# Mamba block with gated FFN on one core: Silu in one instruction and in a burst, the norms' scale on ScalarE, another order on every engine

## What is computed

```
xz = x @ W_xproj.T                     # 64 rank columns, 16 of B, 16 of C
dt = softplus(xz[:64] @ W_dt.T + b_dt)
h_t = exp(dt*A) * h_{t-1} + dt*x*B     # 16 states per channel, a scan over time
y   = sum_s h*C + Dp*x
x1  = layernorm(x + y)
out = layernorm(x1 + (silu(x1 @ Wg.T) * (x1 @ Wu.T)) @ Wd.T)   # 768 hidden columns
```

## Time and profile before

| | |
|---|---|
| median of three executions | 2001.36 us |
| span of the profiled execution | 2000.0 us |
| busy: TensorE, VectorE, ScalarE, GpSimd | 1767, 1828, 1569, 1702 us |
| granted TensorE clock, mean | 0.953 of full |
| moved by DMA | 215.35 MB, 108 GB/s mean |

### The profile page before, as it was taken

The page is one execution under the profiler, slowest core; times in us unless marked ns, Lnnn a source line. Parts: engine busy times, 40 slices in busy tenths (PEclk is TensorE's granted clock), DMA queues, the critical chain, the costliest instruction groups (busy, mean ns, idle before and its releaser), DMA issues.

```text
span 2000.0 us, 37094 instructions
## 1 busy us (share of the span) xinstructions
PE 1766.9 (88%) x11048; PEld 1388.2 (69%) x11048; DVE 1828.2 (91%) x2285; ACT 1568.7 (78%) x2924; POOL 1701.9 (85%) x779
## 2 busy tenths in 40 slices
PE   6788989988899988889888989889989888899886
PEld 3666777676777767777666767667767667777764
DVE  4899999999999999999999999999999999999994
ACT  6878878788877878787788787888777787787862
POOL 5998888988888988889888888988889888889880
PEclk9899999999999999999999999999999999999999
DMA  7233233233233233233233333233333332332300
GB/s 242 89 109 118 94 119 123 90 122 117 86 119 126 87 119 117 96 117 127 85 122 104 110 117 115 97 120 98 117 117 101 111 116 87 117 133 70 122 12 21
DMA packets 116565, 215.35 MB, mean 108 GB/s; under 512 B 11153, under 2 KB 45554, under 8 KB 116466
## 3 DMA queue, kind: packets, MB, share of 16 engines
q1 hardware_dynamic: 116466, 214.40, 32.7%
HBM read 195.48 MB, written 18.87 MB: 107 GB/s over the span
## 4 chain that ended last, share of the span: by engine, by line
PE 51%; issue 19%; DVE 15%; ACT 11%; POOL 2%; DVEq 1%; ACTq 0%; DMA 0%; POOLq 0%; SPq 0%
PE p_o L1005 16%; PE p_y L960 9%; DVE h L705 8%; PE p_m L992 6%; PE p_da L934 5%; PE p_c L943 3%; PE p_m L906 3%; DVE hid L749 3%; PE p_m L914 3%; ACT p_da L539 2%; PE p_m L982 2%; ACT da_k L539 2%; ACT L539 2%; DVE silu_g L743 2%; DVE h L713 1%
## 5 line engine op out<-in xcount | busy, mean ns | idle before, releaser
L422 POOL TENSOR_TENSOR h<-h,c_bc 128x1024 f32<-128x1024 f32 x352 | 832.2, 2368 | 147.6 <-ACT h_carry L525 119.8
L412 POOL TENSOR_TENSOR ub<-u,b_bc 128x1024 f32<-128x1024 f32 x320 | 756.8, 2370 | 0.1
L960 PE MATMUL p_y<-ident,h 128*128 128x128 f32 x4096 | 535.6, 278 | 3.3 <-DVE h L713 2.2
L960 PEld LDWEIGHTS p_y<-ident,h 128*128 128x128 f32 x4096 | 479.9, 144 | 38.5 <-issue 16.4
L539 ACT ACTIVATE p_da<-dt,neg_a 128x512 f32<-128x512 f32 x640 | 432.1, 682 | 86.7 <-DVE h L705 82.8
L705 DVE TENSOR_TENSOR_SCAN h<-p_da,ub 128x512 f32<-128x512 f32 x320 | 380.4, 1210 | 37.9 <-ACT p_da L539 27.4
L705 DVE TENSOR_TENSOR_SCAN h<-p_da,h_carry,ub 128x512 f32<-128x512 f32 x320 | 399.2, 1269 | 11.0 <-ACT p_da L539 10.3
L553 ACT ACTIVATE ub_t<-u_t,bc_t 128x256 f32<-128x256 f32 x768 | 344.9, 497 | 27.7 <-issue 26.9
L1005 PE MATMUL p_o<-wt_down,hid 128*128 128x256 f32 x1536 | 354.7, 381 | 11.8 <-DVE hid L749 8.6
L934 PE MATMUL p_da<-ident,ub_t 128*128 128x128 f32 x1536 | 242.7, 295 | 132.6 <-DVE h L705 131.8
L1005 PEld LDWEIGHTS p_o<-wt_down,hid 128*128 128x128 f32 x1536 | 284.4, 190 | 67.8 <-issue 29.6
(11 more groups left out here) (101 smaller groups left out, 1819.6 us busy)
## 6 DMA issues: line engine op xcount, KB each, us to landing
c_bc<-bc_rows_dram SPq DMA_DIRECT2D x352, 256.0 KB, 4.9
b_bc<-bc_rows_dram SPq DMA_DIRECT2D x128, 512.0 KB, 5.3
x_in<-in_L_attn_x SPq DMA_DIRECT2D x32, 512.0 KB, 3.5
b_bc<-bc_rows_dram SPq DMA_DIRECT2D x64, 256.0 KB, 3.1
out_x<-res_n SPq DMA_DIRECT2D x32, 512.0 KB, 3.3
bc_rows_dram<-bc_rows SPq DMA_DIRECT2D x32, 64.0 KB, 1.6
hid<-in_L_ffn_w_gate SPq DMA_DIRECT2D x1, 768.0 KB, 5.0
hid<-in_L_ffn_w_up SPq DMA_DIRECT2D x1, 768.0 KB, 6.8
```

Source lines behind the costliest of these rows:

```text
L412: nc.gpsimd.tensor_tensor(ub[:, i % UB_SLOTS, :, :], u[:, par, :, :], b_bc[:, i:i + 1, :].broadcast_to([P, DH, T]), ALU.mult).then_inc(s_u ...
L422: nc.gpsimd.tensor_tensor(h[:, s % H_SLOTS, :, :], h[:, s % H_SLOTS, :, :], c_bc[:, i:i + 1, :].broadcast_to([P, DH, T]), ALU.mult).then_i ...
L960: ins = nc.tensor.matmul(p_y_tok[:, k, q * P:(q + 1) * P], h[:, s % H_SLOTS, q, k * P:(k + 1) * P], ident[:, :], start=(s == SUM_ORDER[0] ...
```

## The change

- Silu is one ScalarE instruction that reads the gate block from PSUM and writes `hid` (new `silu`). `silu_of` on VectorE is gone; `hidden` multiplies `hid` in place with the up block.
- TensorE makes all six gate blocks first, in both banks of `p_m` in turn, then all six up blocks, in both banks in turn. The six Silus stand close together on ScalarE, in units 9 and 10, one table load ahead of them and one behind.
- The table loaded at the start and behind the burst holds both Exp and Ln, so softplus needs no load. The norms' scale is exp(-0.5*ln(var+eps)) on ScalarE (`norm_log`, `norm_exp`), the shift one instruction on VectorE (`shifts`); GpSimd's and VectorE's earlier four small ones are gone.
- The decays of K states 6, 10, 14 and 15 are issued two units ahead (`DA_LEAD`), the others still one. The K states are now 2, 6, 9, 10, 14, 15 and the POOL states 0, 1, 2, 3, 4, 7, 9, 10, 11, 13, 14. The counts, six and eleven, are as before.
- All places in `AT` are other ones, TensorE and ScalarE have finer zones, and SyncE (SP) issues the broadcasts in the order in which their buffers come free. The instructions of both norms' last step are spread out (`norm1_0` to `norm1_3`, `norm2_0` to `norm2_3`).

```diff
-POOL_STATES = (0, 2, 3, 4, 5, 8, 9, 10, 11, 12, 14)
+POOL_STATES = (0, 1, 2, 3, 4, 7, 9, 10, 11, 13, 14)
-    "dt_of": (5, 2), "u_of": (8, 0),
+    "softplus_log": (6, 1), "dt_of": (6, 2), "u_of": (5, 1), "u_transposed0": (11, 4), "u_out0": (14, 0),
+    "silu0": (9, 0), "silu1": (9, 1), "silu2": (9, 1), "silu3": (9, 1), "silu4": (9, 3), "silu5": (10, 1),
+    "exp_table": (10, 1), "up0": (10, 1), "up1": (11, 0), "up2": (11, 1), "up3": (13, 2), "up4": (13, 4),
...
-K_STATES = (2, 5, 8, 10, 12, 15)
+K_STATES = (2, 6, 9, 10, 14, 15)
+DA_LEAD = {6: 2, 10: 2, 14: 2, 15: 2}
...
-            def norm_scalars(c):
-
-                wait(pool, s_ln_in, 2 * c)
-                nc.gpsimd.tensor_tensor(rstd[:, :, :], var_eps[:, :, :], neg_half[:, :, :],
-                                        ALU.pow).then_inc(s_rstd, 1)
-                wait(pool, s_rstd, c)
-                nc.gpsimd.tensor_tensor(shift[:, :, :], neg_mean[:, :, :], rstd[:, :, :],
-                                        ALU.mult).then_inc(s_ln, 1)
...
+            nc.scalar.preload_act_table_set("natural_log_exp_and_others")
...
-            def tanh_of(c, j):
+            def silu(c, j, bank=None):
                 act.wait_ge(s_gate_ps, NH * c + (j + 1))
-                nc.scalar.activation(tanh_g[:, :], p_m[:, 0, :], ACT.Tanh,
-                                     scale=0.5 / (QUANT * X1_SCALE)).then_inc(s_tanh, 1)
+                nc.scalar.activation(hid[:, j, :], p_m[:, j % 2, :] if bank is None else bank, ACT.Silu,
+                                     scale=1.0 / (QUANT * X1_SCALE)).then_inc(s_silu, 1)
+
+            def exp_table():
+                nc.scalar.preload_act_table_set("natural_log_exp_and_others")
+
+            def norm_log(call, c1, c2, k=slice(0, 2)):
+                wait(act, s_mean[0], c1)
+                wait(act, s_mean[1], c2)
+                nc.scalar.activation(log_var[:, k, :], mean_var[:, k, :, 1], ACT.Ln,
+                                     bias=eps[:, :]).then_inc(s_log_var, 1)
+
+            def norm_exp(call, k=slice(0, 2)):
+                act.wait_ge(s_log_var, call)
+                nc.scalar.activation(rstd[:, k, :], log_var[:, k, :], ACT.Exp, scale=-0.5).then_inc(s_rstd, 1)
...
-            def silu_of(c, j):
-                wait(dve, s_hid, NH * c + j)
-                dve.wait_ge(s_tanh, NH * c + (j + 1))
-                nc.vector.scalar_tensor_tensor(silu_g[:, :], tanh_g[:, :], 1.0, p_m[:, 0, :],
-                                               ALU.add, ALU.mult).then_inc(s_silu, 1)
...
+            def gate(c, j):
                 pe.wait_ge(s_x1_lo, c + 1)
+                if j >= 2:
+                    pe.wait_ge(s_silu, NH * c + (j - 1))
...
+            def up(c, j):
+                if j >= 2:
+                    pe.wait_ge(s_hid, NH * c + (j - 1))
+                else:
+                    pe.wait_ge(s_silu, NH * c + (NH - 1 + j))
```

More of the change, by code:

```diff
@@ L84, in mamba_ffn_block @@
     assert N - 1 not in POOL_STATES
+    assert all(AT[f"mean{k}"][1] > 0 for k in (1, 2))
     x_chunks = x.rearrange("b (h k p) d -> (b h) p k d", p=P, k=TT)
@@ L164, in mamba_ffn_block @@
         p_m = ps("p_m", [P, 2, T])
-        tail_ps = (p_m, p_da)
-        tail_t = (tanh_g[:, :], ub[:, 0, 0, :])
+        tail_ps = [ps_[:, a, :] for ps_ in (p_m, p_da) for a in range(2)]
         p_m_flat = p_m[:, :, :].rearrange("p a t -> p (a t)")
@@ L208, in mamba_ffn_block @@
         s_da = sem("s_da")
+        s_da_k = [sem(f"s_da_k{q}") for q in range(DH)]
         s_scan = sem("s_scan")
@@ L630, in step @@
                             softplus_log(c + 1, 1 - par)
-                        if prev and due("norm1"):
-                            norm1(c - 1)
+                        for k in range(TT):
+                            if prev and due(f"norm1_{k}"):
+                                norm1(c - 1, k)
                         if prev and due("x1_high"):
                             x1_high(c - 1)
-                        for chunk, j in tiles("tanh", s, zone, 2, c, prev, last):
-                            tanh_of(chunk, j)
@@ L637, in step @@
-                        if last and due("norm2"):
-                            norm2(c - 2, c)
+                        if (prev or last) and due("norm_log"):
+                            norm_log(c, c if prev else 0, c - 1 if last else 0)
+                        if (prev or last) and due("norm_exp"):
+                            norm_exp(c)
+                        for j in range(NH):
+                            if prev and due(f"silu{j}"):
+                                silu(c - 1, j)
+                        if prev and due("exp_table"):
+                            exp_table()
@@ new lines, in step @@
+                        for j in range(NH):
+                            if prev and due(f"up{j}"):
+                                up(c - 1, j)
+                        if zone == 0 and core and s in K_STATES:
+                            ub_transposed(c, s, 1)
+                        if zone == 1:
+                            cb, sb_, pb = unit_at(c, s, -C_LAG, par)
+                            if (core if s >= C_LAG else prev) and sb_ in DVE_STATES:
+                                broadcast_c(cb, sb_, pb)
@@ new lines, in tail_up @@
+            def tail_up(c, j):
+                if j < 4:
+                    pe.wait_ge(s_silu, NH * c + (j + 3))
+                else:
+                    pe.wait_ge(s_hid, NH * c + (j - 3))
+                for n in range(2 * DH):
+                    ins = nc.tensor.matmul(tail_ps[(NH + j) % 4], wt_up[:, n % DH, j * P:(j + 1) * P],
+                                           x1_t[:, n // DH, n % DH, :],
+                                           start=(n == 0), stop=(n == 2 * DH - 1))
+                ins.then_inc(s_up_ps, 1)
@@ L1085, in tail @@
                 for j in range(NH):
-                    tail_gate_up(c, j)
+                    tail_gate(c, j)
+                for j in range(NH):
+                    tail_up(c, j)
                 for i in range(8):
```

322 lines of the change are left out of this document (138 added, 184 removed), and 14 rows, old and new, of the table AT.

## The result

The kernel after takes 1965.15 us (median of four executions, 1960.77 to 1971.19) against 2001.82 before: ratio 0.983 [0.981, 0.985], 37 us faster. Intervals in brackets are of 95%. The forecast was 1920, with a range from 1862 to 1968: the time lies near the slow end of that range, and where 83 us less were forecast, 37 came.

A forecast was written before the change was run, and what follows sets the result against it. VectorE's work plus small waits bounds the period: 53.4 + 3.6 + 0.6 + 0.3 = 57.9 us a chunk against 60.5, -81 us over 31 steps and -2 at the start. Forecast 1920 us, range 1862 to 1968.

The forecast's parts named there:

- VectorE's work: Per chunk on VectorE: six `silu_of` of 0.58 us go, 3.48 us together, so work falls from 56.90 to 53.4 us.
- the softplus' loads: Two table loads around the softplus' Ln on ScalarE go, taking 1.6 us a chunk of VectorE's waits with them.
- Silu's price: On ScalarE, a Silu from PSUM was taken to cost the same as a tanh, 0.60 us; upper bound 1.02 us.
- the start: The first chunk's softplus loses two loads, 2.6 us, nearly all in the start-up chain: -2 us.
- The burst: Two loads and six Silus on ScalarE cost VectorE 3.6 us a chunk: unit 10 1.0, `hidden0` 1.5, scan of 11 1.1.
- Rival D: On ScalarE a table switch costs twice its 1.28 us load: 2.6 us more a burst, 2001 us, no change; chance 0.05.
- E: The change doesn't do what it says: further table loads around the copies, beyond two a chunk; chance 0.01.
- C: Slower: GpSimd becomes the bound through `u` ahead of state 4's product; period 63.2 us, 2085 us; chance 0.05.
- B: TensorE becomes the bound in units 13 to 4: 1.5 us more waits at residuals and `z`, 1967 us; chance 0.13.
- A: The burst is hidden, VectorE keeps 3.54 - 1.6 = 1.9 us of old waits: period 55.3, 1840 us; chance 0.14.
- TensorE's terms from up block 0 on: TensorE's work from up block 0 to `project_dt`, together 32 us, against VectorE's 28 from the scan of 11 to unit 4.
- the other short decay waits: VectorE's remaining short waits for decays in the step, put at 0.3 us a chunk.

## Why the prediction was off

Right, as the traces show it: VectorE's work (53.24 us a chunk for 53.4); the softplus' loads (1.6 us, shown by the kernel before without them); Silu's price (0.60 us like tanh); the start (first `z` at 87.80 in place of 89.98, -2.2 for -2); the tail (45.8 us from the last `z` to the end, 45.7 before). The burst was forecast at 3.6 us of VectorE as 1.0, 1.5 and 1.1; written out it is 1.01, 1.26 and 1.08, 3.34 together. The price of the loads was rightly taken from the earlier trace rows: the drain of 1.38 us that the Trainium skill puts on top of a load ("ScalarE: Activation LUTs", section "What ACT_TABLE_LOAD costs") isn't in the trace of the kernel after either. From the load's start to the Silu behind it are 1000.58 - 999.29 = 1.29 us, and the load starts 0.02 us behind the copy ahead of it. Rival D is out by that, E by the two loads a chunk, C by the missing waits for `ub` outside the return, B since VectorE's waits at the residuals came to 0.86 us a chunk in place of 2.1, and A by the burst's waits. B's 1967 us lies next to the measured time by coincidence: its mechanism isn't what cost the time. Two slips in the working: TensorE's terms from up block 0 on add up to 32.5 us with the costs given there, not 32, and A's 3.54 is 3.59. Neither moves the forecast.

Wrong was this step: "I leave 0.3 for the other short decay waits." Under it lay what the loop's return costs, and the runs show 0.95 us a chunk for that in the kernel after. In the profiled spans the forecast of -83 comes down to the measured -41.0 as follows.
- The loop's returns. Between the first `z` and the last but one there are 30 chunks: 58.98 us each with the loop, 58.03 written out, so 28.5 us. (By the medians the return costs 37; the profiled execution of the kernel after was its fastest, that of the version written out its slowest.) The decay waits at the return were in the table of waits of before, as 13 of the 47 in the earlier trace rows: 15.0 of the 31.6 us, 0.53 a chunk. The softplus' share was 20 waits of 0.67 to 0.68, 0.48 a chunk, not far from the 0.6 that I gave it; the rest I took for small waits of the step. Where the longest of them stand, ScalarE has its 2.05 us of "issue". Two things made the return dearer. One is shown: VectorE's own queue now stops there too. Writing out VectorE's part alone gives back 13 us, ScalarE's and VectorE's together 34. The other is argued only: with less work VectorE may feel a late ScalarE more.
- The last step, from one `z` to the last. I gave it the same gain as all others. Nothing of a next chunk is made there, and the distance between the last two copies of `z` was 52.56 us before. It is 56.08 after, +3.5 in place of -2.6, so 6.1 us. It isn't the loop's: written out, the same distance is 56.45. It isn't fixed either: with GpSimd's part alone written out it is 51.01, and why stays open. In the kernel after VectorE waits 2.3 us for a row of C there, 1.2 for the up block and 1.1 for a decay.
- The base. 60.49 us is the mean of the middle 28 chunks; all 30 give 60.39: 3 us.
- The period itself: 58.03 for 57.9, 4 us. Written out, the residual wait is 0.83 for 0.6, the row of C 0.43 for nothing, the burst 0.3 less, and the decay waits for which 0.3 were left are gone.

28.5 + 6.1 + 3 + 4 = 42, and -83 + 42 = -41. Without the loop's returns in either kernel the change is worth 0.9645 against 0.9964, -64 us.

## What to carry to other kernels

Before a total of waits is put down to a cause, look at where in the program its instances stand: a wait that comes in every second chunk belongs to the loop, not to the step. A loop's return is a price like any other, covered where the bounding engine would have had another wait beside it. A change of order or of work can uncover it, and can make a further engine stop there. Where two engines are late at the same place, curing one gives little (7 and 13 us here) and both much (34).

## What had not been expected of the hardware

- ScalarE stood still for 2.05 to 2.7 us at each of the 13 returns of a loop of 310 to 332 records a pass, waits included, and not at all with 306; with the loop written out no engine stopped at that place.
- VectorE's queue stopped for 2.7 to 3.0 us behind the branch with 333 or 345 records a pass, and for 0.3 us with 335 or 351. The engine showed 0 to 2.2 us of it as idle. TensorE's queue went on within 0.1 us, GpSimd's within 0.3 us.
- A table load in front of another cost just its 1.29 us on ScalarE, and 1.7 us of the kernel's time.
